# A two-layer graph network: loads moved between stages, a softmax stage folded into the next, the sort's halves interleaved

## The reference, cut to what matters

```python
xn = _layernorm(x)
x = x + _L0_gnn_ref(xn, ..., src, dst) + _L0_mix_ref(xn[None], ...)[0]   # sums over edges, by row
x = x + _L0_ffn_ref(_layernorm(x)[None], ...)[0]                         # top 2 of 8 experts
xn = _layernorm(x)
x = x + _L1_gnn_ref(xn, src, dst, ...) + _L1_mix_ref(xn[None], ...)[0]
x = x + _L1_ffn_ref(x, ...)                                              # all 8 experts, weighted

def _L1_gnn_ref(...):   # its end
    h_new = (h_new - mu) * jax.lax.rsqrt(var + LN_EPS) * ln_gamma + ln_beta
    return jax.nn.relu(h_new @ ffn_w + ffn_b)
def _L1_ffn_ref(...):
    w = jax.nn.softmax(feat @ Wr + br, axis=-1)
    ...                 # two layers with batch norm for each expert, then Wo
    return jnp.einsum('bfed,fe->bfd', y, w)
```

## Time and profile before

| what | value |
|---|---|
| median of 3 runs | 6582.67 us (6582.39 to 6586.98) |
| the profiled execution | 6586.9 us |
| its span, first to last instruction | 6585.0 us |
| mean granted clock of TensorE | 0.857 |
| busy: PE, DVE, POOL, ACT | 4899.5, 4371.6, 3473.7, 1839.1 us |

### The profile page before, as it was taken

The page is one execution under the profiler, slowest core; times in us unless marked ns, Lnnn a source line. Parts: engine busy times, 40 slices in busy tenths (PEclk is TensorE's granted clock), DMA queues, the critical chain, the costliest instruction groups (busy, mean ns, idle before and its releaser), DMA issues. The chain is left out here.

```text
span 6585.0 us, 91321 instructions
## 1 busy us (share of the span) xinstructions
PE 4899.5 (74%) x22060; PEld 3601.8 (55%) x22061; DVE 4371.6 (66%) x8953; ACT 1839.1 (28%) x5180; POOL 3473.7 (53%) x3669
## 2 busy tenths in 40 slices
PE   1456766777767774699767777777887868999999
PEld 1345555555555552499534444455555546666665
DVE  8987887878878888733566666667667666333333
ACT  7322322322322322244310000012222216333333
POOL 0117777777777775155157777777777743000000
PEclk8678888888888886799888888887778768999999
DMA  1012222222222222322555555555555533000001
...
DMA packets 383750, 532.66 MB, mean 81 GB/s; under 512 B 123359, under 2 KB 244214, under 8 KB 383478
## 3 DMA queue, kind: packets, MB, share of 16 engines
...
...
## 5 line engine op out<-in xcount | busy, mean ns | idle before, releaser
L877 POOL DMA_INDIRECT got<-table,st_idx x3232 | 3075.4, 952 | 1012.2 <-issue 903.7
L955 PE MATMUL ps_sum<-weighted,hot 128*128 128x260 f32 x6464 | 1853.0, 445 | 178.0 <-DVE acc L1027 173.4
L955 PEld LDWEIGHTS ps_sum<-weighted,hot 128*128 128x128 f32 x6464 | 1387.3, 225 | 594.0 <-DVE acc L1027 264.2
L1027 DVE TENSOR_TENSOR acc<-acc,ps_sum 128x260 f32 x1664 | 705.9, 424 | 745.8 <-PE ps_sum L955 609.4
L940 PE MATMUL ps_score<-score_split,hot_t 128*128 x3232 | 246.3, 184 | 978.9 <-DVE z L1007 952.3
L1019 DVE TENSOR_TENSOR weighted<-got,ps_weight 128x2048 f32<-128x2048 f32 x404 | 921.3, 2280 | 4.3 <-ACT weighted L915 0.8
L940 PEld LDWEIGHTS ps_score<-score_split,hot_t 128*128 128x128 bf16 x3232 | 190.7, 100 | 1160.6 <-issue 1142.0
L912 ACT ACTIVATE ps_weight<-z 128x32 f32<-128x32 f32 x404 | 81.2, 201 | 2655.7 <-DVE z L1007 2655.7
L3056 DVE SCALAR_TENSOR_TENSOR x_res<-ps_yf,comb,x_res 128x256 f32 x392 | 189.6, 484 | 637.9 <-PE ps_yf L2964 637.9
L978 DVE TENSOR_TENSOR hot<-ps_score,row_loc 128x1024 f32<-128x1024 f32 x404 | 491.6, 1217 | 3.5
L2944 PE MATMUL ps_hf<-acc,ws_f 128*128 (+2 forms) x896 | 348.0, 542 | 6.3 <-ACTq L2991 6.3
...
## 6 DMA issues: line engine op xcount, KB each, us to landing
spread<-row_list SPq DMA_DIRECT2D x404, 256.0 KB
got<-table,st_idx POOLq DMA_INDIRECT x3232, 2.8
gate_xin<-ball_rows SPq DMA_DIRECT2D x98, 128.0 KB, 2.3
...
mix_xin<-ball_rows SPq DMA_DIRECT2D x49, 128.0 KB, 2.0
xn_rows<-xs_m SPq DMA_DIRECT2D x49, 128.0 KB, 1.7
```

The lines of the kernel that those rows point to most:

```text
L877: pool.indirect_dma_start(got[:, r, k, :], None, table, bass.IndirectOffsetOnAxis(ap=st_idx[:, r, k:k + 1], axis=0))\
L955: last = nc.tensor.matmul(ps_g[:, p % 2, 0:AW], hot[:, r % 2, k, :], weighted[:, r % 2, k, :], start=(k == n * p), stop=(k == n * p + n - 1))
L1027: nc.vector.tensor_tensor(acc[:, ds(b * AW, AW)], acc[:, ds(b * AW, AW)], ps_g[:, p % 2, 0:AW], ALU.add).then_inc(added, 1)
```

## The change

Four things change.

1. **Sort.** All 1563 real columns are prepared at once. The 28 levels of the low half (1024 columns) and of the high half (640, until now 512 and 128 apart) alternate on VectorE, the high half eight levels behind at the end. Each half has its own semaphore. The wait for the counts' sums comes after all levels.
2. **Experts and entering the second layer.** `TableWeights.load` and its blanking move to the start of `stage_experts` (SP and GpSimd), and after the last result has been written SP loads token group 0 there, into a buffer of its own (`got_y_first`); VectorE collects these two tiles at the end of its list. `stage_l1_enter` starts with groups 1 and 2. The row `k_low` stays in SBUF and is no longer written to DRAM.
3. **Tail weights.** Five of the tail's six weight loads move into pass "_1" (`TailWeights`, issued at `GateMix`'s second lot of loads); the 256-column matrix lands in the free half of `wkv`. Only the broadcast row `b_bc` is loaded in the tail, first in SP's list, and waited for where it is added.
4. **Softmax.** `stage_softmax8` is gone; its five VectorE operations and the exponential stand in `stage_ffn`.

The diff, cut to its core (the body of `collect` is unchanged but for its names):

```diff
-                def runs_of_128(lo, hi):
-                    cur = 0
-                    for k in range(1, 8):
-                        for bit in reversed(range(k)):
-                            if k < 7:
-                                last = exchange_both_ways(keys[cur], keys[1 - cur], lo, hi, k, bit)
-                            else:
-                                last = exchange(keys[cur], keys[1 - cur], lo, hi, bit)
-                            link(last)
-                            cur = 1 - cur
-                    assert cur == 0
+                run_levels = [(k, bit) for k in range(1, 8) for bit in reversed(range(k))]
+                assert len(run_levels) % 2 == 0
+
+                def run_level(h, i):
+                    (lo, hi), (k, bit), (of, to) = SPANS[h], run_levels[i], (keys[i % 2], keys[1 - i % 2])
+                    if i >= 1:
+                        dve.wait_ge(run_done[h], i)
+                    last = exchange_both_ways(of, to, lo, hi, k, bit) if k < 7 else exchange(of, to, lo, hi, bit)
+                    last.then_inc(run_done[h], 1)
+
+                def runs_of_128():
+
+                    n = len(run_levels)
+                    for i in range(n):
+                        run_level(0, i)
+                        if i < n - RUN_BEHIND:
+                            run_level(1, i)
+                    dve.wait_ge(run_done[0], n)
+                    finish(0)
+                    for i in range(n - RUN_BEHIND, n):
+                        run_level(1, i)
+                    dve.wait_ge(run_done[1], n)
+                    finish(1)
...
-                G4 = 12 * P
-                real_keys(0, LOW_G * P)
-                sign_keys(0, LOW_G * P)
-                runs_of_128(0, LOW_G * P)
-                finish(0)
-                real_keys(LOW_G * P, G4)
-                sign_keys(LOW_G * P, G4)
-                runs_of_128(LOW_G * P, G4)
-
+                real_keys(0, EJ)
+                link(nc.vector.memset(keys[1][:, EJ:SORTED].bitcast(I32), LAST_KEY))
+                sign_keys(0, SORTED)
+                runs_of_128()
                 dve.wait_ge(sums, 1)
...
-                real_keys(G4, EJ)
-                link(nc.vector.memset(keys[1][:, EJ:SORTED].bitcast(I32), LAST_KEY))
-                sign_keys(G4, SORTED)
-                runs_of_128(G4, SORTED)
-                finish(1)
...
+class TokenRows:
...
+        self.first = own.enter_context(nc.sbuf_tensor("got_y_first", [P, 2, GROUPS_E[0], D], F32))
...
+    def home(self, p, k):
+        return self.first[:, k, :, :] if p == 0 else self.got[:, p % 2, k, :, :]
+
+    def load(self, sp, p):
+        a, b = self.order.span[p]
+        if p >= 3:
+            sp.wait_ge(self.used, p - 1)
+        whole = min(b, NT - 1)
+        for k in range(2):
+            at = k * NPAD
+            sp.dma_start(self.home(p, k)[:, 0:whole - a, :], self.y_rows[at + a * P:at + whole * P, :].rearrange("(t p) d -> p t d", p=P))\
+                .then_inc(self.y_in[p % 2], 16)
...
+            @block.sync
+            def _(sp):
+                after.load(sp)
+                for r in range(RING):
+                    sp.wait_ge(out[r], 16 * TURNS)
+                tokens.load(sp, 0)
...
+                after.blank()
...
+                tokens.collect(dve, range(tokens.order.span[0][1]))
...
-                load(0)
-                weights.load(sp)
-                load(1)
+                tokens.load(sp, 1)
+                tokens.load(sp, 2)
                 sp.dma_start(wkv[:, :, :], w_qkv[:, D:3 * D].rearrange("(c p) n -> p c n", p=P)).then_inc(wkv_in, 16)
                 for i in range(NTP + 3):
                     p = order.starts(i)
-                    if p is not None and p + 2 < len(order.span):
-                        load(p + 2)
+                    if p is not None and 3 <= p + 2 < len(order.span):
+                        tokens.load(sp, p + 2)
...
-                sp.wait_ge(lowered, 1)
-                sp.dma_start(mix.k_low, small[0:1, :]).then_inc(kept, 16)
...
-                weights.blank()
...
-                collect(range(order.span[0][1]))
...
+class TailWeights:
...
+    def load(self, sp, landed):
+        gamma, beta, w, w_r, b_r = self.of
+        with self.nc.allow_non_contiguous_dma(reason="columns of weights"):
+            sp.dma_start(self.raw, w.rearrange("(c p) n -> p c n", p=P)).then_inc(landed, 16)
+            sp.dma_start(self.gam[:, :], gamma.rearrange("(c p) -> p c", p=P)).then_inc(landed, 16)
+            sp.dma_start(self.bet[:, :], beta.rearrange("(c p) -> p c", p=P)).then_inc(landed, 16)
+            sp.dma_start(self.wl8[:, :, :], w_r.rearrange("(c p) n -> p c n", p=P)).then_inc(landed, 16)
+            sp.dma_start(self.bias8[:, :], b_r.rearrange("(o n) -> o n", o=1).to_broadcast([P, 8])).then_inc(landed, 16)
...
+            mix.tail.load(sp, self.tail_in)
         if self.phase == "last" and r == 1:
+            sp.wait_ge(self.tail_in, 16 * mix.tail.PARTS)
...
-                sp.dma_start(raw[:, :, :], w.rearrange("(c p) n -> p c n", p=P)).then_inc(loaded, 16)
-                sp.dma_start(gam[:, :], gamma.rearrange("(c p) -> p c", p=P)).then_inc(loaded, 16)
-                sp.dma_start(bet[:, :], beta.rearrange("(c p) -> p c", p=P)).then_inc(loaded, 16)
-                sp.dma_start(bb[:, :], b.rearrange("(o n) -> o n", o=1).to_broadcast([P, D])).then_inc(loaded, 16)
...
+                sp.dma_start(bb[:, :], weights.b.rearrange("(o n) -> o n", o=1).to_broadcast([P, D])).then_inc(b_in, 16)
                 load(0)
                 load(1)
                 load_x(0)
                 load_x(1)
-                sp.dma_start(wl8[:, :, :], w_r.rearrange("(c p) n -> p c n", p=P)).then_inc(loaded8, 16)
-                sp.dma_start(bias8[:, :], b_r.rearrange("(o n) -> o n", o=1).to_broadcast([P, 8])).then_inc(loaded8, 16)
...
-                pe.wait_ge(loaded, 64)
...
-                dve.wait_ge(loaded, 64)
...
+                dve.wait_ge(b_in, 16)
...
+                act.wait_ge(dif, 1)
+                nc.scalar.activation(share, share, ACT.Exp).then_inc(exped, 1)
...
+                wide = m[:, :].unsqueeze(2).to_broadcast([P, NT, 8])
+                link(nc.vector.tensor_reduce(m[:, :], share, AX.X, ALU.max))
+                nc.vector.tensor_tensor(share, share, wide, ALU.subtract).then_inc(dif, 1)
...
+                dve.wait_ge(exped, 1)
+                link(nc.vector.tensor_reduce(m[:, :], share, AX.X, ALU.add))
+                link(nc.vector.reciprocal(m[:, :], m[:, :]))
+                link(nc.vector.tensor_tensor(share, share, wide, ALU.mult))
...
-                    stage_softmax8(nc, g, comb)
```

153 lines of the change are left out of this document (68 added, 85 removed).

## The result

The changed kernel takes 6549.09 us (median of 5 runs, 6544.64 to 6551.56) against 6582.67 (5 runs, 6581.42 to 6586.98): 33.6 us less, a ratio of 0.9945 with a 95% interval of 0.9932 to 0.9959. The profiled execution took 6551.56, its span 6549.7; the profiled one of before 6586.9 and 6585.0.

The account below looks back on a forecast made before the run. GpSimd's 3232 row gathers were the costliest group and left alone, so gains came from seams between stages: 15.0 + 11.5 + 7.0 + 4.7 = 38.2 us off, giving 6544 us against the median; range 6535 to 6561 (8 in 10).

Parts of the forecast that it names:

- Part A: Sort: with the wait for the sums behind all levels, the merge starts 15.0 us earlier; ends 11 and 15.4.
- the count ends last: Sort: ScalarE's count finishes after VectorE's levels, by 2.8 us, so VectorE still leaves its wait at 88.51 us.
- sequential bound of 84.8: Sort: VectorE finishes preparation and both halves' levels by 84.8 us even if alternating the halves wins nothing.
- Part D at the head: Second layer's entry: weights and first two tiles loaded earlier let the second token group start at 3186.1, gaining 12.0 us.
- rival 2: Second layer's entry and tail: shared DMA lanes bind, not SP; gains fall to 3 and 4.3 us, time 6555; chance 0.09.
- Part D in the experts' stage: Experts' stage: the 18 weight loads run beside the first gathers and cost 0 to 2 us, taken as 0.5.
- Part D, the key row: End of the second layer's entry: dropping the keys' copy through DRAM gains 0, as it lay beside a longer write.
- Rival 3: Passes: moved buffers change the gathers' pace; 0.012 us a gather loses the whole gain, 0.025 gives 6625 us; chance 0.05.
- Part C: Tail: weights loaded long before end VectorE's 7.11 us wait, only the broadcast row must land; gain 7.0 us, other end 4.3.
- Part B: Softmax ahead of the feed-forward: without its own stage 4.7 us go, at cost 0; ends 3.5 and 5.
- the levels did not end after the count: Denies a sort rival: alternating slows the 56 levels past the count, 0.3 us each costs 14, time 6558; chance 0.10.
- the early loads were early: Denies a rival: a buffer comes free too late, early loads for second-layer entry and tail wait, time 6563; chance 0.04.

Follow-up runs that it names:

- second pair of profiles: The changed kernel and the kernel before, both unaltered, profiled again on one chip: medians 6553.40 against 6590.8 us, ratio 0.9943.
- eight variants: Eight variants of the changed kernel that also load the weights at the start of the experts' stage; that stage takes 424.95 to 426.67 us in them.

## Why the prediction was right, step by step

**Part A** (15.0; measured 15.1 at the merge's start, 15.9 at the stage's end). The step that mattered, "the count ends last", held in three ways: the wait's end stayed at 88.50, halves in sequence changed nothing, and more counting moved the merge by as much. The sequential bound of 84.8 was met to 0.2 us. The 0.9 beyond it lies behind the merge's start and is spread: VectorE's lead over the trace of before moves between 14.5 and 16.5 us within the merge, and the second pair of profiles has 14.5 at the same cut.

**Part D at the head** (12.0; measured 11.9 at the first table row). Every step of the chain came as put: TensorE within 0.04 us of the start, the second group 6.2 behind it where 6.05 was said, and the cover by GpSimd's end held (its 12.45 us are unchanged, VectorE was done at 3167.9, 4 us ahead of the stage). The other end, all token groups landing together at 3190, gave 8 there; it is out, and rival 2 with it.

**Part D in the experts' stage** (0.5; measured 2.6 and 2.3 in the two profiles of the changed kernel, 0.6 to 2.4 in eight variants). The mechanism was right, the value was taken too near the lower of two ends, 0 and 2, and the upper end was short as well. At the start of that stage TensorE waits for the first gathered rows, and SP issues the loads in the stage's first 10 us. They needed to be there only some 400 us later, and asking 17 us later gives all of it back. The prediction's own list of what would show it wrong has "if the experts' stage grows": that sign came, against the line that it is no longer, while its sum had a cost of 0.5 and an end of 2 for it.

**Part D, the key row** (0; measured 0). But the same stretch gained 1.8 us by something that no step had: the write that hid it got faster by a third, by the place of its source. Rival 3 had spoken of "their place" for the gathers; the place counted, for another transfer, and in favour.

**Part C** (7.0; measured 6.4 until VectorE's first product, 4.2 for the stage). The bias row's wait ended at 5387.59, 3.9 us after the stage's start, between the taken 2.6 and the other end, 5.9: 6.4 in place of 7.0. What failed is a step that was not made: who is late next once VectorE no longer waits? Before, VectorE's stall of 7.11 us hid that GpSimd is not ready for an addition until some 10 us after its all-reduce. The trace of before could not show it, for there the addition came 13.55 us after it, a margin of 3 us that nobody knew of. The all-reduce takes 2.3 of the 6.4 back at the first addition's end, and the 4.1 left are the stage's 4.2.

**Part B** (4.7; measured 4.7, less 0.4 to 0.8 in the feed-forward). ScalarE's chain was shorter than put: no table load stands ahead of the root, where before, behind the softmax's exponential, one stood there, and the one load (1.28 us) is followed by the exponential 0.02 us later. So the drain that the Trainium skill (ScalarE: Activation LUTs, What ACT_TABLE_LOAD costs) adds to a switch is not seen here either. (The prediction's estimate from that page, 0.9 us late, counts the drain for one of the two loads in its chain; for both it would have been 2.3.) The 0.6 is TensorE's: its first 16 products take 8.90 us where they took 8.23. The granted clock over 4 us, first before (the stage had begun at 5559.95), then after (begun at 5523.68; columns: window, busy time of PE, PEld, DVE, ACT, POOL, clock, DMA share, GB/s):

```profile
5564.00:5568.00 4.00, 4.00 (x12) 2.15 (x11) 2.60 (x7) 2.10 (x3) 0.00 (x0) 0.96 0.00 0
```

```profile
5528.00:5532.00 4.00, 4.00 (x10) 1.99 (x9) 2.86 (x7) 1.59 (x3) 0.00 (x0) 0.83 0.00 0
```

Both times TensorE began at half the clock (0.50, 1.2 GHz) and rose to 1.00 (2.4 GHz); after the change it rose later against the stage's start, though it had idled for 1.60 us only, and for 6.31 before. Why was not tried.

**The sum.** −38.2 was said, −35.6 was measured between the two profiles, −33.6 between the medians and −37.4 between those of the second pair. The profiled pair's own sum has +2.1 too little cost in the experts' stage, 2.8 too much gain in the tail, 0.6 in the feed-forward and 1.1 in the stages behind the first pass; against it stand 0.9 more in the sort and 3.3 more in the entry stage (1.8 the place of a tile, 1.7 the clock that stayed up, less 0.2 at the head). The passes, which spread over 6 us and 20 us, cancelled in this pair to 0.1; an agreement of a few microseconds is partly luck, and the 3.5 us in the entry stage that no step of the prediction had are luck too. Of the rivals, none came: the levels did not end after the count, the gather's mean stayed, and the early loads were early.
